# Wave attention: four heads' value products in one block, a fourth sine for the last key tile on TensorE, and every angle on VectorE

## The reference, cut to what matters

```
FREQS = [31.0, 37.0, 41.0, 43.0, 47.0]
sim = jnp.einsum('bhid,bhjd->bhij', q, k) / jnp.sqrt(hd) / temp
scores = jnp.zeros_like(sim)
for fi, freq in enumerate(FREQS):
    scores = scores + alpha[:, fi] * jnp.sin(TWO_PI * sim / freq + phi[:, fi])
w = jax.nn.sigmoid(scores)
w = w / (jnp.sum(w, axis=-1, keepdims=True) + 1e-10)
out = jnp.einsum('bhij,bhjd->bhid', w, v)
```

## Time and profile before

| | |
|---|---|
| median of 3 runs | 4277.99 us |
| profiled execution, its own time | 4281.09 us |
| its span | 4279.3 us |
| mean granted clock of TensorE, of full speed | 0.921 |
| TensorE busy, share of the span | 84% |
| VectorE | 80% |
| ScalarE | 67% |
| GpSimd | 30% |

### The profile page before, as it was taken

The page is one execution under the profiler, slowest core; times in us unless marked ns, Lnnn a source line. Parts: engine busy times, 40 slices in busy tenths (PEclk is TensorE's granted clock), DMA queues, the critical chain, the costliest instruction groups (busy, mean ns, idle before and its releaser), DMA issues. The chain is left out here.

```text
span 4279.3 us, 71834 instructions
## 1 busy us (share of the span) xinstructions
PE 3602.2 (84%) x27092; PEld 2304.4 (54%) x27092; DVE 3409.0 (80%) x4519; ACT 2868.0 (67%) x2433; POOL 1271.6 (30%) x918
## 2 busy tenths in 40 slices
PE   3799999999999999999658814999999999998890
PEld 2233333333333333333347814989989889987690
DVE  6899999999999999999465544777777777776662
ACT  3899999999999999999323313555565565654430
POOL 2111111112112121212003343544544544531245
PEclk8899999999999999999869957999999999998895
DMA  5000000000000000000221227222223223312022
GB/s 141 17 12 6 12 12 12 6 12 12 12 9 9 12 12 12 6 12 9 99 71 36 61 65 164 54 47 59 55 45 59 55 45 59 61 31 80 20 64 67
DMA packets 149707, 174.78 MB, mean 41 GB/s; under 512 B 63824, under 2 KB 124848, under 8 KB 141264
## 3 DMA queue, kind: packets, MB, share of 16 engines
q1 hardware_dynamic: 140752, 153.35, 15.5%
q0 software_dynamic: 8704, 17.84, 1.8%
HBM read 119.04 MB, written 52.10 MB: 40 GB/s over the span
## 5 line engine op out<-in xcount | busy, mean ns | idle before, releaser
L704 PE MATMUL psA<-wave,diag 128*128 128x512 f32 x3072 | 1445.5, 622 | 136.5 <-DVE score L860 86.7
L772 ACT ACTIVATE wave<-wave 128x2048 f32<-128x2048 int32 x640 | 1181.2, 1904 | 3.6 <-DVE wave L847 2.2
L704 PEld LDWEIGHTS psA<-wave,diag 128*128 128x128 f32 x3072 | 584.4, 197 | 897.5 <-issue 699.2
L1785 ACT COPY r<-psR 128x1024 f32<-128x1024 f32 x512 | 482.6, 1039 | 358.1 <-PE psR L1709 357.5
L641 POOL TENSOR_TENSOR diag<-ident,par 128x128 f32<-128x128 f32 x384 | 292.6, 788 | 1441.0 <-PE psA L704 1441.0
L1655 POOL COPY kb<-ks 48x2048 bf16<-48x2048 bf16 x128 | 486.4, 3800 | 638.2 <-DMA ks<-kb_parts 534.5
L822 DVE TENSOR_SCALAR wave<-s,par 128x2048 int32<-128x2048 int32 x480 | 612.1, 1275 | 0.0
L847 DVE TENSOR_SCALAR wave<-wave 128x2048 int32<-128x2048 int32 x512 | 609.3, 1215 | 0.0
L1822 DVE TENSOR_TENSOR S<-psR,r 128x1024 f32<-128x1024 f32 x256 | 313.5, 1225 | 290.1 <-PE psR L1724 272.0
L737 ACT ACTIVATE s<-psS,par 128x1024 int32<-128x1024 f32 x256 | 282.8, 1105 | 132.4 <-PE psS L667 132.4
L1794 ACT ACTIVATE W<-psR 128x1024 f32<-128x1024 f32 x256 | 252.2, 1040 | 150.7 <-PE psR L1733 150.7
(11 more groups left out here) (254 smaller groups left out, 4473.7 us busy)
## 6 DMA issues: line engine op xcount, KB each, us to landing
ks<-kb_parts SPq DMA_DIRECT2D x128, 384.0 KB, 5.9
qs<-qb_parts SPq DMA_DIRECT2D x32, 384.0 KB, 8.5
ys<-f_ys SPq DMA_DIRECT2D x36, 256.0 KB
wave_out<-og SPq DMA_DIRECT2D x33, 256.0 KB, 2.1
o<-wave_out SPq DMA_DIRECT2D x8, 1024.0 KB, 5.1
qp<-qa_parts SPq DMA_DIRECT2D x32, 192.0 KB, 3.5
kp<-ka_parts SPq DMA_DIRECT2D x32, 192.0 KB, 4.0
f_wu<-in_w_up SPq DMA_DIRECT2D x2, 2048.0 KB, 10.4
```

Of the source, the lines that this page charges most:

```text
L704: mm = pe.matmul(psA[:, kt, :], diag[:, h % 2, f, :], wave[:, h % 2, f, kt * L:(kt + 1) * L], start=(f == 0), stop=(f == PE_F - 1), skip_g ...
L772: act.activation(wave[:, h % 2, f, :], angle[:, h % 2, f, :], ACT.Sin, scale=float(TWO_PI / 2.0 ** 32)).then_inc(sine, 1)
L1785: act.copy(dst[:, :, k * CP:(k + 1) * CP].rearrange("p h (a n) -> p a h n", a=2), psR[:, n % RING, :, :].rearrange("p a (h n) -> p a h n", ...
```

## The change

There are four edits, all in `wave_attention`:

1. `ACT_LAST` is empty, so VectorE makes the f4 turn of head 0 too.
2. GpSimd makes four diagonals per head, and TensorE adds one product: f3 for the last key tile. So 13 products instead of 12. `summed` is now raised after f2 of the third tile and after f3 of the fourth.
3. VectorE's four additions of 1024 columns become three: f3 on the first three tiles (1536 columns, from `psA`), f4 on the same 1536 columns, and f4 on the last tile (512 columns, from `psA`). The second waits for the first by a semaphore. TensorE's f0 product of the next head waits for the first addition for its tiles 0 to 2 and for the third addition for tile 3.
4. The value products of all four heads of the earlier group stand in one block, behind the sine products of head 1. Within it the order is key tile outside, head inside, so four heads with different output partitions follow each other.

The description also speaks of sigmoids inside a head. The diff holds no edit of `sigmoids` or of its place.

```diff
-ACT_LAST = (0,)
+ACT_LAST = ()
...
-                        for f in range(PE_F):
+                        for f in range(ALL_F):
                             ins = pool.tensor_tensor(diag[:, h % 2, f, :], ident[:],
...
-            def values(g, slot, heads):
...
+            def values(g, slot):
+                pe.wait_ge(v_ready, g + 1)
+                pe.wait_ge(out_taken, g + C_TAKEN)
+                pe.wait_ge(weighed, g * HG + HG)
                 for kt in range(QT):
-                    for h in heads:
+                    for h in range(HG):
...
-                        for f in range(PE_F):
+                        for f in range(ALL_F):
                             pe.wait_ge(sine, n * NF + f + 1 + C_SINE)
-                            for kt in range(QT):
-                                if f == 0 and kt % 2 == 0:
-
-                                    pe.wait_ge(added, n * ADDS - ADDS + kt // 2 + 1 + C_ADDED)
+                            for kt in range(QT) if f < PE_F else (QT - 1,):
+                                if f == 0 and kt in (0, QT - 1):
+
+                                    pe.wait_ge(added, n * ADDS - ADDS + (1 if kt == 0 else ADDS) + C_ADDED)
+                                final = f == (PE_F if kt == QT - 1 else PE_F - 1)
                                 mm = pe.matmul(psA[:, kt, :], diag[:, h % 2, f, :],
                                                wave[:, h % 2, f, kt * L:(kt + 1) * L],
-                                               start=(f == 0), stop=(f == PE_F - 1), skip_group_check=True)
-                                if f == PE_F - 1 and kt % 2 == 1:
+                                               start=(f == 0), stop=final, skip_group_check=True)
+                                if final and kt >= QT - 2:
                                     mm.then_inc(summed, 1)
...
-                        if h in (0, 2):
-                            values(g, 1 - u, (h, h + 1))
+                        if h == VALUES:
+                            values(g, 1 - u)
...
+            def add_sines(n, u, h):
+                most, rest = slice(0, MOST), slice(MOST, N)
+                sums = psA[:].rearrange("p a n -> p (a n)")
+                dve.wait_ge(sine, n * NF + PE_F + 1 + C_SINE)
+                dve.wait_ge(summed, n * 2 + 1 + C_SUMMED)
+                add_sine(n, u, h, PE_F, most, sums[:, most])
+                dve.wait_ge(sine, n * NF + NF + C_SINE)
+                dve.wait_ge(added, n * ADDS + 1 + C_ADDED)
+                add_sine(n, u, h, NF - 1, most, score[:, u * HG + h, most])
+                dve.wait_ge(summed, n * 2 + 2 + C_SUMMED)
+                add_sine(n, u, h, NF - 1, rest, sums[:, rest])
```

More of the change, by code:

```diff
@@ L27 @@
 PE_F = 3
+ALL_F = 4
 TWO_PI = 2.0 * float(np.pi)
@@ L549, in wave_attention @@
     SR, AR = 2, 2 * HG
-    DV_F = NF - PE_F
-    ADDS = 2 * DV_F
+    VALUES = 1
+    ADDS = 3
+    MOST = (QT - 1) * L
     C_SPS, C_SREADY, C_TURNED, C_LAST, C_CUT, C_SINE, C_USED, C_SUMMED = 2 * 2 * HG, 2, 2 * HG * (NF - 1), 2 * HG, 2 * HG * NF, NF, 2 * PE_F, 4
@@ L565, in wave_attention @@
         far = sb(c, "far", [P, 1], I32)
-        diag = sb(c, "diag", [P, 2, PE_F, P])
+        diag = sb(c, "diag", [P, 2, ALL_F, P])
         og = sb(c, "og", [P, L])
@@ L682, in values @@
                                        start=(kt == 0), stop=(kt == QT - 1), skip_group_check=True)
-                if heads[-1] == HG - 1:
-                    mm.then_inc(out_ps, 1)
+                mm.then_inc(out_ps, 1)
             def pair(gg, last):
@@ L722, in _ @@
             pair(NG // 2 - 1, True)
-            for h in (0, 2):
-                values(NG, 1, (h, h + 1))
+            values(NG, 1)
         @block.scalar
@@ L835, in make_angles @@
                     elif f < NF:
-                        dve.wait_ge(added, n * ADDS - 2 * ADDS + 2 * (f - PE_F + 1) + C_ADDED)
+                        dve.wait_ge(added, n * ADDS - 2 * ADDS + (1 if f == PE_F else ADDS) + C_ADDED)
                     if (f or general) and (f < NF - 1 or (f == NF - 1 and (general or h not in ACT_LAST))):
@@ L848, in make_angles, with add_sine @@
                                           ALU.logical_shift_left).then_inc(cut, 1)
[L850 to L863, removed]
+            def add_sine(n, u, h, f, cols, other):
+                dve.scalar_tensor_tensor(
+                    out=score[:, u * HG + h, cols], in0=wave[:, h % 2, f, cols],
+                    scalar=par[:, u, 1, h * NF + f:h * NF + f + 1], in1=other,
+                    op0=ALU.mult, op1=ALU.add).then_inc(added, 1)
+            def add_sines(n, u, h):
[9 more added lines that the diff above has]
+                add_sine(n, u, h, NF - 1, rest, sums[:, rest])
             def pair(gg, last, general):
@@ L877, in pair @@
                             dve.wait_ge(out_ps, g + C_OUT)
-                        for f in range(PE_F, NF):
-                            add_sine(n, u, h, f)
+                        add_sines(n, u, h)
             dve.tensor_scalar(far[:], bound[:], FAR * min(FREQS) / HD, None, ALU.is_ge).then_inc(far_ready, 1)
```

## The result

The changed kernel takes 4416.53 us (median of 4 runs) against 4279.68 for the kernel before in the same comparison: ratio 1.0323, interval 1.0304 to 1.0342, 137 us slower. The profiled executions are 4413.48 and 4281.09 us, 132.4 apart.

What follows compares the result with a forecast made beforehand. The ring through TensorE and ScalarE was to bound the kernel: links of 31.5, 16.2 and 14.7 us plus 0.85 for the clock make 63.25 per group, 2.53 more, times 31 = 78 us: 4356, range 4290 to 4420.

Steps and rivals of the forecast that it cites:

- the ring: Chain of waits from VectorE's additions through TensorE and ScalarE and back; forecast to bound the group at 63.25 us.
- rival 1: The forecast itself (0.75): the ring through TensorE and ScalarE becomes the bound; own range 4306 to 4417 us.
- both heads slow: Case of the forecast: TensorE's clock always falls in heads 0 and 1, 64.1 us per group, 4383 in all.
- VectorE's work: VectorE's own time: 14.7 us per head, 58.8 per group against 59.77, so 0.95 shed, including 0.14 for the chained addition.
- third link: From VectorE's additions of head 2 past head 3 to head 0: VectorE's work stands, 14.7 us to head 3.
- Value block: Value products of four heads behind head 1: 32 records forecast to overlap fully and take 3.54 us.
- Rival 2: Four heads don't overlap beyond two, so the value block takes 7.1 us: 4466 us in all (chance 0.08).
- Second link: From VectorE's additions of head 1 to head 2, through TensorE with the value block: 16.2 us against VectorE's 14.7.
- the clock: TensorE's clock falls behind waits: head 1 taken as always slow, head 0 in half the groups, adding 0.85 us.
- the first link: From VectorE's additions of head 3 past head 0 to head 1: 30.7 us, or 31.5 with head 1's clock fall.
- Rival 3: VectorE stays the bound and the kernel gets faster: 58.8 us per group, at best 4218 us (chance 0.12).
- ScalarE's 1.99 us: ScalarE loses head 0's f4 turn, 1.99 us per group; forecast as no gain, since ScalarE already waits for scores.

Runs made afterwards that it cites:

- e4: Changed kernel with filler products in TensorE's waits, 2 ahead of f0 of head 0 and 5 ahead of head 1's: 61.80 us per group, 1.0088 of the kernel before.
- e5: Changed kernel with the four sigmoids moved from behind head 0 into head 1, behind its third sine: 60.33 us per group, 0.9965 of the kernel before.
- e10: Changed kernel with 5 filler products ahead of f0 of head 1 alone: 62.18 us per group, 1.0112 of the kernel before.
- e11: Kernel before, none of the four edits, with 2 filler products ahead of f0 of heads 0 and 1 each: 60.03 us per group, 0.9965 of it unfilled.
- e6: Changed kernel with sigmoids moved into head 1 and the value block cut by key tiles behind heads 1 and 2: 59.20 us per group, 0.9889 of the kernel before.

## Why the prediction was right, and where it was off

- **Direction and mechanism: right.** VectorE's own work shrank and the ring became the bound. The waits stand where they were forecast: before the additions of heads 1 (4.11 us, forecast 1.3 to 3.8) and 2 (0.97, forecast 1.5), none in 3 and 0. e4 and e5 confirm it from two sides. The size was 137 us against 78, since a group takes 64.84 and not 63.25. The time lies only 3 us inside the range, and that is partly luck: the upper end of rival 1 was made of a dearer value block, which didn't come, while both heads slow at the forecast's prices gave 4383.
- **VectorE's work.** A head without a wait is 1052.67 - 1037.94 = 14.73 (forecast 14.7). The chained addition starts 0.04 after its predecessor's end (1039.78 against 1037.94 + 1.80). The third, which waits for neither of them, starts 0.08 before the second's end (1041.52). That is 0.12, forecast 0.14. The Trainium skill ("VectorE: DVE Perf Modes", "The DRAIN you can't avoid") says that the semaphore costs nothing, measured there on tensor copies; here it is off by this 0.12. VectorE as a whole sheds much less than the 0.95 of the forecast: its busy time falls from 1736.53 / 29 = 59.88 to 59.63 us per group. Most of the difference is the slower instructions in heads 1 and 2, see the third link.
- **Value block.** Forecast 3.54, measured 1076.76 - 1073.21 = 3.55 for 32 records. Rival 2 is out. 32 records at 0.43 would be 13.8 us, so the four run 3.9 times as fast as one. The Trainium skill's 3.07 times ("TensorE: Matmul & The Clock Gate", "Part 3: Packing small matmuls — row/col tiling") is measured there for four row tiles, and these are four column tiles; the estimate that the prediction drew from it, 4.5 us, didn't come.
- **Second link: right,** 16.18 against 16.2, and TensorE's wait ahead of head 1 is 4.68 against 4.9.
- **The term that was mis-sized: the clock in the first link.** The link is 33.66 against 31.5 + 0.85. Head 0's f0 was to be slow in half of the groups; it is slow in all 31, 5.24 instead of a mean of 4.5. Head 1's f0 takes 5.99 to the scores and not 5.32, since it is slow from its first record: the granted clock is 0.50 from 1058.00 on, ahead of its start at 1058.77, while in the group of the earlier trace rows it was still 1.00 up to 1063.50, 1 us into f0. These are 0.8 and 0.7 us of the missing 1.6. e10 shows why the half was a poor guess: the fall in head 0 depends on what stands in head 1, so a share counted in the old schedule doesn't carry over.
- **The first link before the change.** The prediction put it at 29.5 to 30.3 us, hidden behind VectorE's 30.5. (By its own terms it is 29.3 to 30.1.) That leaves out the groups in which head 0 is slow too. In one of them the link took 831.42 - 799.84 = 31.58 us, and e11 shows that the slow f0 cost 0.69 us per group already before. So the ring was hidden only in some groups, and VectorE's idle 0.85 us came from the others.
- **Third link: 15.02 against 14.7,** 0.3 more; the other terms came out 0.15 shorter in sum. In the two heads where VectorE waited, its second addition takes 1.92 instead of 1.82 and the turn behind 1.48 instead of 1.27, with GpSimd's diagonals starting beside the additions (1073.36 and 1089.54). I had costed GpSimd at nothing. That GpSimd is the cause wasn't tested.
- **Rival 3 (VectorE stays the bound)** asked for both links to be shorter than summed. They aren't in this kernel. They are in e6, with the sigmoids inside a head, as the change's own words say and its diff doesn't, and the value block in halves: 0.9889. The prediction held that with the sigmoids moved rival 3 would be right. The move alone isn't enough: in e5 the second link stays at the value block's length (0.9965, a period of 60.33 and not 58.8).
- **ScalarE's 1.99 us at nothing: right.** Its wait for scores grew from 97.6 to 251.9 us.

## What to carry to other kernels

When the busiest engine is 98% busy, look for the second-longest ring of waits and how far it is behind before taking work off the first: here it was 1 us of 60 or less. Work put on another engine is free only in the heads where that engine is ahead. A block moved out of a wait into a stretch where its engine is the late one adds its full length to that engine's path there, and the wait that it leaves behind can slow the engine's clock besides. A long block of one table's work belongs where its engine has already delivered what others wait for.

## What the hardware showed unexpectedly

- Behind an unchanged 2.04 us wait of TensorE in head 0, the clock fell in every group of the changed kernel, and in 7 of 31 of e10, where only the wait of another head was filled.
- Filler products that do nothing useful made the changed kernel faster by 3.04 us of 64.84 per group, and the kernel before by 0.35% (ratio 0.9965, 0.9951 to 0.9979).
- Four products into four groups of 32 output partitions ran beside each other with no loss that shows: 3.55 us for 32 records, as two of them do for 16.
